# Queries from split half-precision rows and weights, normalised on ScalarE; biases added by GpSimd in the FFN; the first expert's weights split in the tail

## The reference

```python
# block 0 and block 1, cross-attention (16 heads of 16); context has 375 rows per item
x = x + gate * (softmax(mask(norm(x) @ Wq @ K.T / 4)) @ V @ Wo + b_o)   # K, V from the context
# block 0, FFN: weights of +1 and -1, features 256 -> 1024 -> 1024 -> 256
x = x + gate * s2 * (relu(s1 * (relu(s0 * (h @ k0)) * 2) @ k1) * 2) @ k2   # h = [norm(x), -norm(x)]
# block 1, FFN: 8 experts (256 -> 1024 -> 256, relu), each token goes to one, at most 448 tokens each
x = x + gate * p[token] * expert[e[token]](norm(x))
```

## Time and profile before

| | us |
|---|---|
| median of 3 runs (lowest 1647.42, highest 1654.29) | 1648.17 |
| the profiled execution | 1659.43 |
| its span | 1657.2 |
| setup | 0 to 29.3 |
| attention of layer 0 | 29.3 to 539.9 |
| FFN | 546.5 to 875.4 |
| attention of layer 1 with its tail | 875.4 to 1463 |
| experts | 1463 to 1657.2 |

### The profile page before, as it was taken

How to read it: one execution, slowest core, us unless ns; L and a number is a source line. 1 busy time by engine, 2 the same in 40 slices (tenths; PEclk the granted TensorE clock), 3 DMA queues, 4 the chain that set the end, 5 groups by cost and what they waited for, 6 DMA issues and landing times.

```text
span 1657.2 us, 40853 instructions
## 1 busy us (share of the span) xinstructions
PE 1485.0 (90%) x15435; PEld 1081.2 (65%) x15435; DVE 1079.0 (65%) x3580; ACT 818.5 (49%) x1907; POOL 854.5 (52%) x904
## 2 busy tenths in 40 slices
PE   0889999999998599999996699999999899759994
PEld 0457778777886355666664377777777666537773
DVE  5877777777775455555555677777777777336661
ACT  3456666666665222222222367666667565424441
POOL 0077777777776000000000477778888777744341
PEclk9999999999999799999998899999999999969997
DMA  5764544555440242222226655655676553044430
GB/s 146 206 134 102 105 103 102 103 102 102 104 85 19 59 152 70 65 63 63 64 79 162 178 106 116 116 111 114 130 141 135 98 94 59 26 149 152 146 101 8
DMA packets 214603, 172.73 MB, mean 104 GB/s; under 512 B 70026, under 2 KB 207695, under 8 KB 214408
## 3 DMA queue, kind: packets, MB, share of 16 engines
q1 hardware_dynamic: 208776, 160.35, 42.3%
q0 software_dynamic: 5632, 9.78, 2.0%
HBM read 95.86 MB, written 41.15 MB: 83 GB/s over the span
## 4 chain that ended last, share of the span: by engine, by line
PE 55%; DMA 4%; DVE 3%; POOL 1%; issue 1%; ACT 1%; SPq 1%; POOLq 0%; DVEq 0%; ACTq 0%
PE bank L1754 14%; PE bank L1942 5%; PE bank L1017 5%; PE bank L1928 5%; PE bank L1047 4%; PE bank L1065 4%; PE bank L953 4%; PE bank L974 4%; PE bank L1765 3%; DMA q_stack_a<-max_t_a 1%; PE bank L1097 1%; PE bank L1043 1%; DMA xg_f<-x_after_attention 1%; DVE max_parts_a L1391 1%; PE bank L1073 1%
## 5 line engine op out<-in xcount | busy, mean ns | idle before, releaser
L1202 ACT ACTIVATE probs_a<-bank 125x448 f32<-125x448 f32 x768 | 384.5, 540 | 17.2 <-PE bank L1047 7.9
L825 POOL TENSOR_TENSOR probs_a<-probs_a,mask_keep 125x448 int32<-125x448 int32 x256 | 285.4, 1138 | 97.0 <-ACT probs_a L1202 96.8
L1382 DVE CUSTOM_DVE_ANT_0 masked_scores_a<-bank,mask_add_a 112x375 bf16<-112x375 f32 x512 | 262.6, 546 | 107.6 <-PE bank L1017 107.0
L825 POOL TENSOR_TENSOR probs_a<-probs_a,keep_a 125x448 int32<-125x448 int32 x256 | 285.9, 1137 | 84.0 <-ACT probs_a L1202 82.8
L1382 DVE CUSTOM_DVE_ANT_0 masked_scores_a<-bank,mask_add 112x375 bf16<-112x375 f32 x512 | 260.5, 549 | 75.0 <-PE bank L1017 71.3
L1017 PE MATMUL bank<-k_stack_a,q_stack_a 96*128 96x375 f16 x1024 | 293.0, 326 | 17.4 <-DVE row_max_a L1382 16.2
L1047 PE MATMUL bank<-q_stack_a,k_stack_a 97*128 97x224 f16 x1536 | 253.3, 260 | 6.3 <-DMA q_stack_a<-max_t_a 5.5
L890 POOL TENSOR_TENSOR ctx_low_a<-ctx_in_a,ctx_high_a 128x375 f16<-128x375 f32 x128 | 113.1, 905 | 164.3 <-ACT ctx_high_a L1180 164.2
L1047 PEld LDWEIGHTS bank<-q_stack_a,k_stack_a 97*128 97x128 f16 x1536 | 146.9, 98 | 66.4 <-DMA q_stack_a<-max_t_a 6.4
L1754 PE MATMUL bank<-h0h_f,ffn_w 128*128 128x448 f16 x512 | 181.6, 355 | 0.0
L1754 PE MATMUL bank<-h0l_f,ffn_w 128*128 128x448 f16 x512 | 181.4, 354 | 0.0
(11 more groups left out here) (217 smaller groups left out, 3201.0 us busy)
## 6 DMA issues: line engine op xcount, KB each, us to landing
k_stack_a<-k_high_a SPq DMA_DIRECT2D x256, 96.0 KB, 4.0
ctx_in_a<-in_ctx_dram SPq DMA_DIRECT2D x64, 375.0 KB, 3.6
w_in_e<-in_L_ffn_W_dram SPq DMA_DIRECT2D x14, 1024.0 KB, 8.5
k_stack_a<-k_low_a SPq DMA_DIRECT2D x128, 96.0 KB, 4.2
q_stack_a<-q_split SPq DMA_DIRECT2D x128, 84.0 KB, 3.5
q_split<-high_a SPq DMA_DIRECT2D x32, 224.0 KB, 3.8
mask_in_f<-in_mask_BxSxS_if_dram SPq DMA_DIRECT2D x8, 656.2 KB, 6.9
mask_keep<-keep_f SPq DMA_DIRECT2D x8, 656.2 KB
```

The lines of the kernel that those rows point to most:

```text
L825: pool.tensor_tensor(bits, bits, cols, ALU.mult).then_inc(masked, 1)
L1202: act.activation(probs[:, i, :], score_bank[i % 3][0:CK, 0:GT], ACT.Exp, scale=DK ** -0.5).then_inc(exped, 1)
L1382: dve.tensor_tensor_reduce(masked_scores[:, use_of[x.value, h] % 3, :], bank_of(x, h)[0:S, 0:S2], mask_add[x.four][:, 0:S2], 1.0, -LARGEST ...
```

## The change

- Queries: `wq` is split in the setup like wk and wv, and the turned rows `xt` into `xt_high` (ACT) and `xt_low` (DVE, new `low_rows`). Where four single-precision products made a group's queries, twelve half-precision ones do (high x high, high x low, low x high). The normalisation moves from DVE to ACT (new `normalise`, four activations with a scale and a bias per row), for which DVE makes `shift`. `low_rows` stands at the end of DVE's call.
- Biases: the matmul L1094 with `pick` and `bias` is gone. POOL adds layer 0's bias to each item of `xg` when it has been loaded in the FFN, and layer 1's bias to a second copy of the FFN's result, which it stores in a new tensor `x_and_bias_1`; layer 1's `x_sum` is loaded from it. SP loads x of FFN group s only when that second store of group s-2 has landed (`based_stored`).
- Start of layer 1: the clearing of pads and tables, with its waits for stores, moves into step 1 (`prepare`), behind q2 and q3; `low_rows` of group 0 is done at the end of the FFN.
- First expert's weights: loads in steps 33 to 36 (two pieces each), high parts in steps 38 to 41, low parts in steps 39 to 42.

```diff
@@ setup_phase: wq is split too; pick and bias are gone
-            for w in "kvqo":
+            for w in "qkvo":
...
-            act.wait_ge(raw_loaded, 64)
+            act.wait_ge(raw_loaded, 96)
@@ class Queries, def vector(self, dve, s)
             dve.wait_ge(self.dev_ready, p + 1)
+            wait(dve, self.xn_ready, p)
             dve.reciprocal(self.scale[:, :], self.dev[:, :]).then_inc(self.scaled, 1)
...
-            for b in range(G):
-                last = dve.tensor_scalar(self.xn[p % 2][:, b, :], self.xg[p % 2][:, b, :], self.mean_var[:, b, 0:1],
-                                         self.scale[:, b:b + 1], ALU.subtract, ALU.mult)
-            last.then_inc(self.xn_ready, 1)
+            dve.scalar_tensor_tensor(out=self.shift[:, :], in0=self.mean_var[:, :, 0], scalar=-1.0, in1=self.scale[:, :],
+                                     op0=ALU.mult, op1=ALU.mult).then_inc(self.shifted, 1)
...
+        if 0 <= p < NG and not (self.layer and s == 1):
+            self.low_rows(dve, p)
+
+    def low_rows(self, dve, p):
+        for c in range(KC):
+            dve.wait_ge(self.xt_high_ready, KC * p + c + 1)
+            dve.tensor_tensor(self.xt_low[p % 2][:, c, :], self.turn_bank[p % 2][c][:, 0:GT],
+                              self.xt_high[p % 2][:, c, :], ALU.subtract).then_inc(self.xt_low_ready, 1)
+
+    def normalise(self, act, p):
+        act.wait_ge(self.shifted, p + 1)
+        if p > 1:
+            act.wait_ge(self.turned, KC * (p - 1))
+        for b in range(G):
+            last = act.activation(self.xn[p % 2][:, b, :], self.xg[p % 2][:, b, :], ACT.Identity,
+                                  bias=self.shift[:, b:b + 1], scale=self.scale[:, b:b + 1])
+        last.then_inc(self.xn_ready, 1)
@@ def scalar(self, act, s)
+        if 0 <= p < NG:
+            self.normalise(act, p)
         if 0 <= q < NG:
...
@@ def tensor(self, pe, s)
-            pe.wait_ge(self.xt_ready, KC * (q + 1))
+            pe.wait_ge(self.xt_low_ready, KC * (q + 1))
...
+                high, low = self.m["wq"][self.layer]
+                xt_high, xt_low = self.xt_high[q % 2], self.xt_low[q % 2]
                 for c in range(KC):
-                    last = pe.matmul(self.q_bank(q, j)[:, 0:GT], self.m["wq"][self.layer][:, c, j * P:(j + 1) * P],
-                                     self.xt[q % 2][:, c, :], start=c == 0, stop=c == KC - 1)
+                    for n, (w, part) in enumerate(((high, xt_high), (high, xt_low), (low, xt_high))):
+                        last = pe.matmul(self.q_bank(q, j)[:, 0:GT], w[:, c, j * P:(j + 1) * P], part[:, c, :],
+                                         start=c == 0 and n == 0, stop=c == KC - 1 and n == 2)
@@ attention_phase
     def load_beside(sp, s):
-        if layer and 20 <= s < 28:
-            experts.load_first(sp, s - 20)
+        if layer and 33 <= s < 37:
+            experts.load_first(sp, 2 * (s - 33))
+            experts.load_first(sp, 2 * (s - 33) + 1)
...
     def high_beside(act, s):
-        if layer and 28 <= s < 32:
+        if layer and 38 <= s < 42:
...
     def low_beside(dve, s):
-        if layer and 28 <= s < 32:
+        if layer and 39 <= s < 43:
...
-                sp.dma_start(x_sum[d.four][:, :], take(x_in, d.value)).then_inc(x_loaded[d.four], 16)
+                sp.dma_start(x_sum[d.four][:, :], take(x_rest, d.value)).then_inc(x_loaded[d.four], 16)
...
-            pe.matmul(work_bank[0:S, 0:D], m["pick"][:, :], m["bias"][layer][:, :], start=True, stop=False)
...
+            if layer and s.value == 1:
+                prepare()
@@ ffn_phase: SP, POOL, DVE
-                wait(sp, y_ready, G * (s.back(2).value + 1) if s.back(2).exists(NG) else 0)
+                wait(sp, based_stored[s.slot], 16 * s.pair)
                 sp.dma_start(xg[s.slot][:, :, :], take(x_rows, s.value)).then_inc(x_loaded[s.slot], 16)
...
+            if s.exists(NG):
+                pool.wait_ge(x_loaded[s.slot], 16 * (s.pair + 1))
+                for b in range(G):
+                    pool.tensor_tensor(xg[s.slot][:, b, :], xg[s.slot][:, b, :], m["bo"][0][:, :],
+                                       ALU.add).then_inc(x_based, 1)
             if p.exists(NG):
-                hold(pool, y_ready, G * (p.value + 1), passed)
+                for b in range(G):
+                    pool.wait_ge(y_ready, G * p.value + b + 1)
+                    pool.tensor_tensor(xg[p.slot][:, b, :], y[p.slot][:, b, :], m["bo"][1][:, :],
+                                       ALU.add).then_inc(y_based_ready, 1)
                 pool.dma_start(take(out_rows, p.value), y[p.slot][:, :, :]).then_inc(stored[p.slot], 16)
+                pool.wait_ge(y_based_ready, G * (p.value + 1))
+                pool.dma_start(take(based_rows, p.value), xg[p.slot][:, :, :]).then_inc(based_stored[p.slot], 16)
...
-            dve.wait_ge(x_loaded[s.slot], 16 * (s.pair + 1))
             for b in range(G):
+                dve.wait_ge(x_based, G * s.value + b + 1)
                 last = dve.bn_stats(stats[:, b, :], xg[s.slot][:, b, :])
...
+            if s.value == NG:
+                after.queries.low_rows(dve, 0)
```

More of the change, by code:

```diff
@@ L176, in flamingo_program @@
             "sign": sb("sign", [P, 2], F32),
-            "wq": [sb(f"wq{n}", [P, KC, D], F32) for n in range(2)],
+            "wq": [[sb(f"wq{n}_{part}", [P, KC, D], F16) for part in ("high", "low")] for n in range(2)],
             "wk": [[sb(f"wk{n}_{part}", [P, KC, D], F16) for part in ("high", "low")] for n in range(2)],
@@ L180, in flamingo_program @@
             "wo": [sb(f"wo{n}", [P, KC, D], F32) for n in range(2)],
-            "bias": [sb(f"bias{n}", [P, D], F16) for n in range(2)],
-            "pick": sb("pick", [P, S], F16),
+            "bo": [sb(f"bo{n}", [S, D], F32) for n in range(2)],
             "mask_add": sb("mask_add_0", [S, S2 + P - CK], BF16),
@@ L284, in _ @@
             dve.memset(m["eps"][:, :], EPS)
-            dve.memset(m["pick"][:, :], 0.0).then_inc(blank, 1)
-            for n in range(2):
-                dve.memset(m["bias"][n][:, :], 0.0).then_inc(blank, 1)
-            dve.wait_ge(blank, 3)
-            for row in (0, LOW):
-                dve.memset(m["pick"][row:row + 1, :], 1.0)
             dve.wait_ge(small_loaded, 80)
@@ L371, in __init__ @@
         self.xn = [sb(f"xn{n}", [S, G, D], F32) for n in range(2)]
-        self.xt = [sb(f"xt{n}_q", [P, KC, GT], F32) for n in range(2)]
+        self.xt_high = [sb(f"xt_high{n}_q", [P, KC, GT], F16) for n in range(2)]
+        self.xt_low = [sb(f"xt_low{n}_q", [P, KC, GT], F16) for n in range(2)]
+        self.shift = sb("shift_q", [S, G], F32)
         self.high = [sb(f"high{n}", [P, KC, GT], F16) for n in range(2)]
@@ L445, in vector @@
                 dve.wait_ge(self.high_ready, KC * q + c + 1)
-                dve.tensor_tensor(self.low[q % 2][:, c, :], self.q_bank(q, c)[:, 0:GT],
-                                  self.high[q % 2][:, c, :], ALU.subtract).then_inc(self.low_ready, 1)
+                dve.scalar_tensor_tensor(out=self.low[q % 2][:, c, :], in0=self.q_bank(q, c)[:, 0:GT], scalar=1 / W_SCALE,
+                                         in1=self.high[q % 2][:, c, :], op0=ALU.mult,
+                                         op1=ALU.subtract).then_inc(self.low_ready, 1)
         if s < NG:
             dve.wait_ge(self.x_loaded[s % 2], 16 * (s // 2 + 1))
-            wait(dve, self.xn_ready, s)
+            wait(dve, self.shifted, s)
             for b in range(G):
@@ L466, in scalar @@
                 act.wait_ge(self.q_ready, KC * q + c + 1)
-                act.activation(self.high[q % 2][:, c, :], self.q_bank(q, c)[:, 0:GT], ACT.Copy).then_inc(self.high_ready, 1)
+                act.activation(self.high[q % 2][:, c, :], self.q_bank(q, c)[:, 0:GT], ACT.Copy,
+                               scale=1 / W_SCALE).then_inc(self.high_ready, 1)
         if 0 <= p < NG:
@@ L1101, in project @@
                     last = pe.matmul(work_bank[0:S, 0:D], part[:, c, :], w[:, c, :],
-                                     start=False, stop=c == KC - 1 and n == 2)
+                                     start=c == 0 and n == 0, stop=c == KC - 1 and n == 2)
             last.then_inc(projected, 1)
@@ L1314, in vector, with prepare @@
[L1314 to L1329 removed]
+        def prepare():
+            if layer:
+                for n in range(2):
+                    dve.wait_ge(ffn.stored[n], 16 * NG // 2)
+                    dve.wait_ge(ffn.based_stored[n], 16 * NG // 2)
+                    dve.wait_ge(ffn.add_stored[n], 16 * NG // 2)
+                    dve.wait_ge(ffn.keep_stored[n], 16 * NG // 2)
+            dve.memset(max_parts[:, :, HH:], 0.0)
+            if not layer:
+                dve.tensor_scalar(wo_high[:, :, :], m["wo"][layer][:, :, :], W_SCALE, None, ALU.mult).then_inc(wo_split, 1)
+                dve.wait_ge(wo_split, 1)
+                dve.scalar_tensor_tensor(out=wo_low[:, :, :], in0=m["wo"][layer][:, :, :], scalar=W_SCALE,
```

(16 more changed lines are left out.)

91 lines of the change are left out of this document (31 added, 60 removed).

## The result

| | us |
|---|---|
| before, median of 4 runs (1647.42 to 1662.11) | 1651.23 |
| after, median of 4 runs (1679.78 to 1683.81) | 1681.65 |
| ratio, 95% interval | 1.0183 (1.0146 to 1.0219) |
| span of the profiled executions, before and after | 1657.2, 1682.0 |

The change makes the kernel slower by 30 us. The forecast was 1655.9, slower by 7.7, with a range to 1669: the sign was right and the time lay outside the range.

What follows compares the result with a forecast made beforehand. PE, busy 90% of the span, bounds attention and DVE paces the query calls; setup +0.7, queries +16.6, layer 1 start +12, FFN +2, bias matmul -6.5, splits -19.6, tail +2.5 gave +7.7 on 1648.2: 1655.9 us, range 1638 to 1669.

Steps and rivals of the forecast that it cites:

- tail +2.5: Tail: ACT's and DVE's splits placed there delay the last item and some POOL operations, +2.5 us (0.5 to 6).
- FFN +2: FFN: POOL's bias adds cost +1.8 at the first group and are hidden from group 3 on, +2 us (1 to 10).
- queries 2.2 + 16.6: Setup's extra loads and splits delay ACT and DVE by 2.2; layer 0's query calls at 8.1 add 16.6 us.
- start of layer 1 +12: Start gains about 0, clearing in step 1 costs +4.4, and slower query calls bring it to +12 us (7 to 16).
- With the splits gone these steps go back to 14.6: 78.1 - 58.5 = -19.6: Layer 1, steps 28 to 31: DVE's long stalls go with the splits, -19.6 us (-20 to -13).
- I carry the difference over as it is: Whole kernel: the median run's 11.3 us below the profiled one stays unchanged, so 1648.2 + 7.7.
- 60 of the 64 lie in steps that PE fills: Attention steps: removing the bias matmul, 0.108 us each, saves PE time directly, -6.5 us (-7 to 0).
- The long stall did not turn up elsewhere: Rival: the splits' stall returns in other steps, three times 6.5 us, giving 1675; chance 0.06.
- the clock did not stay up: Rival, query calls: PE stays at full clock, a call takes 7.2, -8.7 us, giving 1647; chance 0.17.
- ACT did hold DVE: Rival, query calls: ACT's normalisation does not hold DVE, a call stays 5.2, giving 1631; whole or half, chance 0.12.
- rivals on POOL in the FFN: Rival, FFN: POOL late through the lock or slow stores, six groups lose 1.5 each, +10, giving 1666; chance 0.07.
- bias matmul that gives nothing: Rival, attention steps: the matmul's time is covered by a later wait, giving 1662; chance 0.10 together with the tail rival.

Runs made afterwards that it cites:

- e1: Kernel before with only the first expert's splits and loads moved into the tail: 1640.85 us, ratio 0.9943.
- e9: Kernel before with the change's bias parts and the first expert's splits in the tail: 1646.54 us, ratio 0.9963.
- e11: Kernel before with the negation of the maxima as scalar_tensor_tensor instead of tensor_scalar, splits left in place: 1653.85 us, ratio 0.9993.
- e15: Kernel before with only DVE's low parts of the first expert moved into the tail (steps 39 to 42): 1643.04 us, ratio 0.9937.
- e2: Kernel before with only the biases changed: matmul out, POOL's adds and second store in, clearing of pads not moved: 1658.12 us, ratio 1.0064.
- e7: Changed kernel without the third product (low weights by high rows), eight matmuls instead of twelve: ratio 1.0122.
- e4: Changed kernel with the four normalisations back on DVE, split rows and weights kept: 1670.11 us, ratio 1.0131.
- e5: Changed kernel with `low_rows` ahead of the statistics in DVE's call, ACT still normalising: ratio 1.0135.
- e8: Kernel before with splits in the tail and the clearing of expert_in behind the loads of FFN group 2: 1636.28 us, ratio 0.9909.
- e12: Kernel before with splits in the tail, clearing of expert_in behind group 2's loads, and the negation as scalar_tensor_tensor: 1638.13 us, ratio 0.9904.
- e10: Kernel before with biases, splits in tail, POOL's group 1 adds later, bias store first, expert_in clearing behind group 2's loads: 1637.04 us, ratio 0.9910.
- e14: Kernel before with biases, splits in tail, the three FFN mends, and the clearing of pads moved into step 1: 1637.23 us, ratio 0.9904.

## Why the prediction was wrong

By the ratios the change falls into three parts: splits (e1), biases on top (e9 less e1), queries and clearing on top (after less e9). The intervals leave 3 to 6 us to each. By the medians alone, taken on different chips in part, the rows would be -9.2, +5.7 and +35.1.

| us | predicted | measured |
|---|---|---|
| splits: -19.6, tail +2.5 | -17.1 | -9.4 |
| biases: matmul -6.5, FFN +2, setup -1.5 | -6.0 | +3.3 |
| queries 2.2 + 16.6, start of layer 1 +12 | +30.8 | +36.3 |
| sum | +7.7 | +30.2 |

**Splits.** The step that failed is here, and it is the largest error of a single term. The trace agrees with the step in its own execution: -18.9 in steps 28 to 31, +3.1 in the tail. What failed was the step "With the splits gone these steps go back to 14.6: 78.1 - 58.5 = -19.6" as a price for ordinary runs. One profiled execution with three stalls was read as every execution, and "I carry the difference over as it is" was the warning passed by: the profiled one lay 11.3 above the median. The saving of 9.4 with the tail's 3 says that an ordinary run holds some 12 us of such stalls, not 19.6. That the stalls come with the splits and end with POOL's run was right and is shown (e1, e11, e15).

**Biases.** A second step failed here: "60 of the 64 lie in steps that PE fills". The matmul gave 0.11 a step as priced in ordinary steps of both layers (31 steps of layer 0: -2.6, and -3.5 in e2; 14.44 instead of 14.55 in layer 1), but the 23 first steps of layer 1 gave 0.4 together: some of them ran 0.5 to 1.6 long. It is no accident of this pair: the 23 steps take 336.4 to 338.7, 337.4 in the mean, in the seven profiles with the matmul, and 334.2 to 340.7, mean 337.1, in the eleven without it, four of which have a second step of 17.4 to 19.8. Which wait takes the gain was not found. In the FFN the term was +2 and the trace has +6.6: 1.7 for the adds ahead of the first statistics, as predicted (+1.8); 1.2 for the collision of DVE with POOL, which stood only as a rival; 3.6 at group 2, which the text allowed for ("may get 4 worse or 1 better") and then counted at almost nothing. From group 3 on the chain was hidden as predicted: phases of 38.7.

**Queries.** The working of a call held: 2.07 for the normalisations (2.1), DVE idle 2.7 (2.6), twelve products in 4.45 at half clock (4.5), a call 7.85 and 8.16 (8.1), 7.2 where PE does not delay it (e7). But the text named one cause, the normalisation, and the chain through PE at half clock only as a correction; e4 and e5 show the two to be worth about as much. The prediction took the clock rule of the Trainium skill (TensorE: Matmul & The Clock Gate, Part 1), that an idle array falls to the 1.2 GHz level, as every call slow at 8.6. The trace agrees that the level falls behind a pause, and not that it does in each call: 0.50 over one call's products and 1.00 over another's, 0.77 over the calls, which take 7.03 to 8.7. What was short stands around these calls. In layer 0 the setup took 2.1 more where +0.7 stood (up to q1's scale; 0.5 to 0.8 more in the traces of the six runs made from the changed kernel), q2 and q3 took 4.0 where 2.9 stood, and the four calls gave 1.1 of that back; the last call q8, which has no statistics but the whole wait, took 3.0, as priced. In layer 1 the same call took 3.3, and only +1.1 was put there. In layer 0 some 2.2 more came at the first score units: the small instruction of the long stalls waited 2.52 there for POOL instead of 1.78, PE paused 1.47 instead of 0.73, and behind that pause it ran at half clock, which took another 1.4 (a window of the changed kernel there):

```profile
115.80:119.00 3.20, 3.13 (x14) 2.15 (x15) 0.56 (x2) 0.03 (x1) 3.13 (x2) 0.51 1.19 157
```

The start of layer 1 was right: q2's statistics start 12.2 after the last add, before 12.25, now held by x, which lands 12.15 behind that add instead of 9.7. From the last add to q4's scale it takes 5.2 more where +4.4 stood, for the clearing.

**Rivals.** The long stall did not turn up elsewhere, the clock did not stay up, and ACT did hold DVE. The rivals on POOL in the FFN and on a bias matmul that gives nothing each named a part of what went wrong, at 0.07 and within 0.10; the tail was near its term (3.1 for 2.5), though the part behind step 31 scatters as much, 275.0 to 278.4 in the four profiles with the splits in place and 277.5 to 281.2 in the others. Several of them at once was a case that the range left out.

## What to carry to other kernels

A stall that the trace shows once or thrice can differ from run to run (3, 2, 1 and 3 of them in four profiles here): when the profiled execution lies well off the median, price what you remove by the median run too, or remove it alone and time that. When work in a software pipeline goes to another engine, follow every loop of the call and not only the engine that gets the work: here a loop through ACT and one through half-clock matmuls each set the pace, and mending one showed little until both were. And look at the order of issue on a queue: the kernel before, its splits moved, got some 5 us faster by putting a 3.6 MB fill behind a 448 KB load.

The fastest versions stand level, at 0.990 to 0.991: the splits in the tail and the clearing behind the loads (e8, e12), with or without the mended biases (e10, e14).

## What the runs showed of the hardware

A small DVE instruction (8 columns, operands in SBUF) waited 4.8 us, through the rest of five masks, a root and two more masks on POOL, and ended 0.03 us behind the last, in either of two forms (e11). The Trainium skill (SBUF — State Buffer, two separate sides) has the shared port pair locked for a whole instruction; here the wait went over several, which these runs show and do not explain. It is not always so: at the first items of the kernel before, the same instruction, from 94.40 on, was let in behind a single memset of POOL (L908), which ended at 96.15, and ended itself at 96.18, ahead of POOL's next memset at 96.21. The records of the masks overlap by some 0.06, and those of the memsets stand 0.06 apart. Four DVE normalisations took 2.60 instead of 1.38 beside POOL's adds (1.79 to 2.61 in other profiles with the same adds), and 1.38 again when the adds were put off (e10). A 448 KB store took 10.6 to land beside a 3.6 MB fill and 3.9 ahead of it; as the second of two such stores without a fill it took 5.1.
